# Layer 1 attention: values made in the projection, first maximum packs awaited by row group, key packs issued half a step sooner

## The chip, the cores and the metric

The kernel runs on one core of one Trainium2 chip. The metric is the time on the device in microseconds. An engine of the core is TensorE (PE, its weight loads are PEld), VectorE (DVE), ScalarE (ACT), GpSimd (POOL) or SyncE (SP); SP issues all DMAs of this kernel.

## The reference, cut to what matters

Two transformer layers run one after the other on 2 x 1024 tokens of width 128: attention, normalization, a mixture of experts, normalization, twice. The change is in the attention of layer 1, with 16 heads of 8 channels:

```
q = x @ W_q
k = x @ W_k
v = x @ W_v
latent_kv = (k + v) @ W_down_kv
k_rec = (latent_kv @ W_up_k).reshape(b, s, H, HD).transpose(0, 2, 1, 3)
v_rec = (latent_kv @ W_up_v).reshape(b, s, H, HD).transpose(0, 2, 1, 3)
scores = jnp.einsum('bhqd,bhkd->bhqk', qh, k_rec) / math.sqrt(d)
decay = jnp.exp(-LAMBDA_DECAY * jnp.abs(t[:, None] - t[None, :]))
attn = jax.nn.softmax(scores * decay[None, None, :, :], axis=-1)
out = jnp.einsum('bhqk,bhkd->bhqd', attn, v_rec)
```

## The kernel before

**Projection** (project_l1, line 868). The tokens are taken in four groups of 512. PE makes queries (line 922), the sum of keys and values (918, 919), its 32 latent rows (931) and the keys (935). ACT copies the sum and the latent out, the latent into a part of PR, the tile that later holds the exponentials. DVE multiplies queries and keys by the two decay factors (983; four planes w for each group), and every plane is cut into three bf16 parts: ACT rounds the first (949), DVE subtracts it (988), ACT rounds the second (953), POOL makes the third (998). For groups 0 and 1, which are batch 0, this ends here and SP writes the parts to DRAM (q_parts, k_parts; 895). For groups 2 and 3 only the first part is made, and the rests stay in PR (`rest`); second and third parts follow in the attention (1424 and 1281, tile `late`).

After the first and second parts have landed, SP's program for the projection issues the key and query packs of the first maximum step (`mp.load_k`, 12 DMAs, lines 1065 and 1068, tile KM; `mp.load_q`, 8 DMAs, line 1055, tile QM) and then eight stores of third parts (895). The projection is a block of its own: no engine begins the next block before all engines have ended theirs.

**Attention** (attention_l1, line 1072). An *iteration* `it` (0 to 7) is four heads of one batch; a *half step* `h` (0 to 15) is one half of its queries, and `h = 2 it` is the even one. In each half step there are NT = 9 groups `g` of four heads, so g runs from 0 to 143. PE makes the scores of a group (1347) from the packs QP and KP, ACT takes the exponential (1434) into PR, POOL masks the diagonal (1290), and two groups later PE multiplies by the values V (1366) into OUT. The row maximum that goes into the exponent is made ahead: for each half step 16 *maximum tiles* of 128 x 1024 products on PE (1316) that DVE reduces at once (1446); DVE negates and splits the 16 columns (1455, 1458), PE turns them (1325), DVE copies them out (1467, tile MT), and SP writes them as two rows into QP (1190, `max_rows(h)`). The first scores of half step h wait for these rows, and those of an even one also for the packs. PE runs 22 maximum tiles (LEAD) before the first scores, then two in most groups.

**In these 22 tiles** PE also makes the values: 16 blocks of 128 tokens by 144 columns, three in one PSUM bank, so six fills (`values`, 1375), which ACT copies into V (1420). After them it runs 56 products of the identity by itself that nothing reads (`keep_busy`, 1381).

**SP's queue in the attention** has one order: wait for the stored third parts, rows of ones for KP (1231), the packs KP (5 DMAs, 1178) and QP (6 DMAs, 1166) of iteration 0, QM of iteration 1, `max_rows(0)`, KM of iteration 1, `max_rows(1)`. Then for each half step h: the stored sums of h-1 (1195), fetches of earlier results (1205, 1207) and inverses (1214, 1220), in an even half step QP of the next iteration (6 DMAs), in an odd one its KP (5 DMAs; for iteration 1 both in half step 0), then `max_rows(h + 1)`, late parts, and in an even half step QM and KM of the iteration after the next (20 DMAs).

Of the kernel before, what the change touches and what calls it, by code (L numbers as in the profile page):

```python
# [22 lines left out]
ALU = mybir.AluOpType  # L23
# [844 lines left out]
def project_l1(nc, X, t, mp, late, PR, QS, KS):  # L868

    NV = 4  # L870
    with ExitStack() as ctx:
        sb, pb, sem = sbuf(nc, ctx), psum(nc, ctx), Sems(nc, ctx)
        W, DEC = t["W"], t["DEC"]
        lat, rest = PR[0:DL + 1, 2].rearrange("p j c -> p (j c)"), PR[:, 0:2].rearrange("p s w c -> p w s c")
        loaded, dec_loaded, first_stored, stored = (t[n] for n in ("loaded", "dec_loaded", "first_stored", "stored"))
        kv = sb("p1_kv", [P, TOK], F32)
        val = sb("p1_val", [P, NV, 2, GW], F32)
        early = sb("p1_early", [P, NV, NPART, S], BF16)
        psQ, psKV, psK = ([pb(f"p1_{n}{s}") for s in range(2)] for n in ("psQ", "psKV", "psK"))
        psL = pb("p1_psL")  # L880
        q_ready, kv_ready, kv_read, lat_ready, lat_read, k_ready, val_done, rest_done, part1, part2, part3, ones_set = (
            sem(f"p1_{n}") for n in ("q_ready", "kv_ready", "kv_read", "lat_ready", "lat_read", "k_ready",
                                     "val_done", "rest_done", "part1", "part2", "part3", "ones_set"))
# [4 lines left out]
        def part(g, w, i):  # L888
            return (early, late)[g // 2][:, w, i, g % 2 * GW:(g % 2 + 1) * GW]

        with nc.Block() as block:  # L891
            @block.sync
            def _(sp):
                def store(g, w, i, done):
                    sp.dma_start((QS if w < 2 else KS)[:, w % 2, i, :, grp(g)], part(g, w, i)).then_inc(done, 16)

                for g in range(2):
                    for w in range(NV):
                        for i, written in enumerate((part1, part2)):
                            sp.wait_ge(written, g * NV + w + 1)  # L900
                            store(g, w, i, first_stored)
                sp.wait_ge(first_stored, 2 * NV * 2 * 16)
                mp.load_k(sp, 0)
                mp.load_q(sp, 0)
                for g in range(2):
                    for w in range(NV):
                        sp.wait_ge(part3, g * NV + w + 1)
                        store(g, w, 2, stored[0])

            @block.tensor  # L910
            def _(pe):
# [11 lines left out]

                first(0)
                for g in range(NG):
                    if g + 1 < NG:
                        first(g + 1)
                    pe.wait_ge(kv_read, g + 1)
# [6 lines left out]
                    nc.tensor.matmul(psK[g % 2][:], W["upk"][:], lat[0:DL, grp(g)], start=True, stop=True).then_inc(k_ready, 1)  # L935

            @block.scalar
            def _(act):
# [15 lines left out]

                copy_kv(0)
                for g in range(NG):
# [3 lines left out]
                    else:  # L960
                        first_part(g, 0)
                    if g + 1 < NG:
                        copy_kv(g + 1)
# [6 lines left out]
                    if g < 2:  # L970
                        second_part(g, NV - 1)

            @block.vector
            def _(dve):
                dve.wait_ge(dec_loaded, 16)
                for g in range(NG):
                    pos = slice((g % 2) * GW, (g % 2 + 1) * GW)
                    for w in range(NV + 1):
# [5 lines left out]
                        if w:  # L984
# [7 lines left out]
            def _(pool):  # L992
                nc.gpsimd.memset(lat[DL:DL + 1, :], 1.0).then_inc(ones_set, 1)
                pool.wait_ge(ones_set, 1)
                for g in range(2):
                    for w in range(NV):
                        pool.wait_ge(part2, g * NV + w + 1)
                        nc.gpsimd.tensor_tensor(part(g, w, 2), rest[:, w, g % 2], part(g, w, 1), ALU.subtract).then_inc(part3, 1)

# [35 lines left out]
class MaxPacks:  # L1035


    Q_LOADS, K_LOADS = 8 * 16, 12 * 16

    def __init__(self, nc, ctx, QS, KS):  # L1040
# [5 lines left out]
        self.k_loaded = [sem(f"km_loaded{s}") for s in range(2)]  # L1046

    def load_q(self, eng, it):

        b, q, s = it // NQUAD, it % NQUAD, it % 2  # L1050
        for g in GROUPS:
            heads = slice(q * HQ + g // 2 * 2, q * HQ + g // 2 * 2 + 2)
            for r in range(2):
                rows = slice(g * MROWS + r, (g + 1) * MROWS, 2)
                eng.dma_start(self.Q[s][rows].rearrange("r h a t -> r (h a) t"), self.QS[heads, :, 0:2, :, b * S:(b + 1) * S].rearrange("h a i d t -> (i d) (h a) t"))\
                    .then_inc(self.q_loaded[s], 16)

    def load_k(self, eng, it):

        b, q, s = it // NQUAD, it % NQUAD, it % 2  # L1060
        for g in GROUPS:
            heads = slice(q * HQ + g // 2 * 2, q * HQ + g // 2 * 2 + 2)
            tok = slice(b * S + g % 2 * GW, b * S + (g % 2 + 1) * GW)
            r0 = g * MROWS
            eng.dma_start(self.K[s][r0:r0 + MROWS:2].rearrange("r h a t -> r (h a) t"), self.KS[heads, :, 0:2, :, tok].rearrange("h a i d t -> (i d) (h a) t"))\
                .then_inc(self.k_loaded[s], 16)
            for i in range(2):
                eng.dma_start(self.K[s][r0 + 1 + i * 2 * HD:r0 + (i + 1) * 2 * HD:2].rearrange("r h a t -> r (h a) t"), self.KS[heads, :, 1 - i, :, tok].rearrange("h a d t -> d (h a) t"))\
                    .then_inc(self.k_loaded[s], 16)


def attention_l1(nc, t, mp, late, PR, ones16, QS, KS, OD, RD, OC):
# [15 lines left out]
    FILL = GW // VW  # L1088
    NFILL = -(-B * KB // FILL)
# [9 lines left out]
    def tiles_until_turn(h):  # L1099

        return issued(turn_group(h) - 1) if h else NTILE + 2
# [3 lines left out]
    def tile_slot(m):  # L1105

        return m + sum(tiles_until_turn(h) <= m for h in range(NHALF))

# [25 lines left out]
    with ExitStack() as ctx:  # L1134
# [3 lines left out]
        COR, ID, WV, stored = (t[n] for n in ("COR", "ID", "WV", "stored"))  # L1138
        V = sb("a1_V", [P, B * KB, VW], F32)
        lat, rest = PR[0:DL + 1, 2].rearrange("p j c -> p (j c)"), PR[:, 0:2].rearrange("p s w c -> p w s c")  # L1140
        junk = sb("a1_junk", [P, 2, S], BF16)
        OST = [sb(f"a1_OST{s}", [P, GW], F32) for s in range(2)]
        SPREAD = sb("a1_SPREAD", [P, 2, GW], F32)
# [11 lines left out]
        ones_loaded, out_clear, s_filled, s_read, m_filled, m_read, masked, pv_done, out_read, neg_done, m_rows, inverse_done, scaled, mid_done, low_done, v_ready, v_kept = (  # L1155
            sem(n) for n in ("ones_loaded", "out_clear", "s_filled", "s_read", "m_filled", "m_read", "masked", "pv_done", "out_read",
                             "neg_done", "m_rows", "inverse_done", "scaled", "mid_done", "low_done", "v_ready", "v_kept"))
# [24 lines left out]
        with nc.Block() as block:  # L1182
            @block.sync
            def _(sp):
# [7 lines left out]
                def store(h):  # L1192

                    sp.wait_ge(out_read, h + 1)
                    sp.dma_start(OD[h], OST[h % 2][:]).then_inc(out_stored[h % 2], 16)
# [32 lines left out]

                sp.wait_ge(stored[0], 2 * 4 * 16)
# [3 lines left out]
                load_pack_q(sp, 0)  # L1233
                mp.load_q(sp, 1)
                max_rows(0)
                mp.load_k(sp, 1)
                max_rows(1)
                for h in range(NHALF):
# [11 lines left out]
                    if it + 1 < NIT:  # L1250
# [4 lines left out]
                        if h % 2 == (it >= 1):  # L1255
# [40 lines left out]
            def _(pe):  # L1296
# [5 lines left out]
                def max_tile(m):  # L1302
                    h, i, k = m // NTILE, m % NTILE, tile_slot(m)
                    it, s = h // 2, h // 2 % 2
                    row, j = h % 2 * 4 + i // HQ, MAX_ORDER[i % HQ]
                    if h % 2 == 0 and i == 0:
                        pe.wait_ge(mp.q_loaded[s], (it // 2 + 1) * mp.Q_LOADS)
                        pe.wait_ge(mp.k_loaded[s], (it // 2 + 1) * mp.K_LOADS)
# [61 lines left out]
                def values(f):  # L1370

                    if f >= NRING:
                        pe.wait_ge(v_kept, f - NRING + 1)
                    for n in range(f * FILL, min(f * FILL + FILL, B * KB)):
                        last = nc.tensor.matmul(ring[f % NRING][:, n % FILL * VW:(n % FILL + 1) * VW], lat[:, n * P:(n + 1) * P], WV[:],
                                                start=True, stop=True)
                    last.then_inc(v_ready, 1)

                def keep_busy(n):

# [548 lines left out]
```

## Time and profile before

| | |
|---|---|
| median of 3 runs | 1486.66 us (1485.92 to 1486.88) |
| the profiled execution | 1490.03 us, its span 1488.3 us |
| PE busy | 1293.4 us (87% of the span) |
| DVE busy | 1131.8 us (76%) |
| ACT busy | 907.9 us (61%) |
| POOL busy | 476.7 us (32%) |
| mean granted TensorE clock | 0.932 |
| layer 1 projection | 749 to 794 us of the span |
| layer 1 attention | 794 to 1227 us |

Times of the trace count from the span's start. An engine's idle time is put before the instruction that ended it, with the releaser. PEclk is 1.00 at 2.4 GHz and 0.50 at 1.2 GHz. A row of SPq is the issue of a DMA and not its transfer; "landing" is the time from a DMA's issue to its completion. A wait for several semaphores is put down to one of them.

### The profile page before, as it was taken

How to read it: one execution, taken by the hardware profiler on the slowest of the kernel's cores; microseconds unless marked ns; L12 is line 12 of the kernel's file. 1: busy time of each engine (PE TensorE's matmuls, PEld its weight loads, DVE VectorE, ACT ScalarE, POOL GpSimd, SP SyncE). 2: the span in 40 equal slices, each digit the busy share in tenths (PEclk: the TensorE clock that was granted, in tenths of full speed). 3: DMA queues.
4: the chain of work that ended last, by engine and by line, in shares of the span. 5: the costliest groups of instructions: out<-in, count | busy, mean ns of one | idle time of the engine just before them, and what ended most of it. 6: DMA issues, size and time to landing. Idle time of an engine off the chain costs nothing. (4 is left out here: it accounts for less than half of the span.)

```text
span 1488.3 us, 23429 instructions
## 1 busy us (share of the span) xinstructions
PE 1293.4 (87%) x7928; PEld 736.6 (49%) x7928; DVE 1131.8 (76%) x1741; ACT 907.9 (61%) x1502; POOL 476.7 (32%) x988
## 2 busy tenths in 40 slices
PE   4299889608999999999876999899999968999998
PEld 1133333406778778787623222232222316877776
DVE  4266766287999999999665788788898736688885
ACT  3188887104555555555442487788888854767774
POOL 4254545003333343433132242244223422121210
PEclk9599999758999999999985899999999998999999
DMA  4423230005666666666227075443442201022200
GB/s 136 123 54 103 56 102 8 7 14 132 152 147 154 141 156 145 155 148 146 97 78 153 19 160 133 117 102 93 112 113 62 59 26 59 6 99 82 85 29 29
DMA packets 72157, 141.09 MB, mean 95 GB/s; under 512 B 13132, under 2 KB 45197, under 8 KB 65133
## 3 DMA queue, kind: packets, MB, share of 16 engines
q1 hardware_dynamic: 72048, 139.72, 37.5%
q8 instruction: 59, 0.97, 0.3%
q14 instruction: 50, 0.40, 0.1%
HBM read 121.55 MB, written 16.82 MB: 93 GB/s over the span
## 5 line engine op out<-in xcount | busy, mean ns | idle before, releaser
L1446 DVE CUSTOM_DVE_ANT_0 a_junk<-a_mring,a_COR 128x1024 bf16<-128x1024 f32 x256 | 303.5, 1218 | 61.3 <-PE a_mring L1316 60.8
L1434 ACT ACTIVATE a_PR<-a_ring 128x512 f32<-128x512 f32 x576 | 299.9, 603 | 70.9 <-PE a_ring L1347 70.7
L1290 POOL TENSOR_SCALAR_AFFINE_SELECT a_PR<-a_PR 128x128 f32<-128x128 f32 x512 | 136.4, 297 | 267.6 <-ACT a_PR L1434 267.1
L811 ACT ACTIVATE e_HH<-e_H 128x512 fp32r<-128x512 f32 x184 | 116.5, 633 | 162.5 <-DVE e_H L859 162.4
L1347 PE MATMUL a_ring<-a_QP,a_KP 74*128 74x512 bf16 (+3 forms) x768 | 177.7, 334 | 11.6 <-DMA a_KP<-k_parts 6.2
L415 DVE TENSOR_SCALAR a_PR<-a_PR,a_lo,a_hi 128x1024 f32<-128x1024 f32 (+1 forms) x160 | 122.0, 774 | 77.1 <-ACT a_PR L389 74.4
L389 ACT ACTIVATE a_PR<-a_ring,a_ng 128x1024 f32<-128x1024 f32 (+1 forms) x160 | 155.0, 1033 | 14.8 <-PE a_ring L318 14.1
L1366 PE MATMUL a_OUT<-a_PR,a_V 128*9 128x512 f32 (+3 forms) x1536 | 153.0, 495 | 0.0
L830 DVE TENSOR_TENSOR e_HL<-e_H,e_HH 128x512 fp32r<-128x512 f32 x138 | 140.8, 1021 | 13.2
L1347 PEld LDWEIGHTS a_ring<-a_QP,a_KP 74*128 74x128 bf16 x768 | 57.0, 98 | 168.1 <-ACT a_PR L1434 123.1
L1716 DVE TENSOR_TENSOR e_HL<-e_GL,e_HH 128x512 fp32r<-128x512 f32 x144 | 108.4, 757 | 38.2 <-ACT e_HH L1684 34.5
L753 POOL TENSOR_TENSOR e_HL<-e_H,e_HH 128x512 fp32r<-128x512 f32 x46 | 78.8, 1712 | 181.6 <-ACT e_HH L811 181.6
L291 POOL TENSOR_SCALAR_AFFINE_SELECT a_PR<-a_PR 128x128 f32<-128x128 f32 x256 | 98.5, 410 | 110.6 <-DVE a_PR L415 110.6
L1677 ACT ACTIVATE e_GL<-e_psF,e_BF 128x512 f32<-128x512 f32 x144 | 99.2, 690 | 54.2 <-PE e_psF L1635 53.9
L859 DVE TENSOR_TENSOR e_H<-e_T,e_ROUTE 128x512 f32<-128x512 f32 x176 | 122.1, 694 | 1.5
L853 DVE TENSOR_TENSOR e_T<-e_SG,e_psU 128x512 f32<-128x512 f32 x176 | 119.4, 678 | 1.2 <-PE e_psU L769 1.1
L804 ACT ACTIVATE e_SG<-e_psG 128x512 f32<-128x512 f32 x184 | 108.6, 590 | 16.5 <-PE e_psG L769 16.4
L1316 PE MATMUL a_mring<-a_KM,a_QM 32*128 32x512 bf16 (+3 forms) x704 | 80.9, 336 | 20.9 <-PEq L891 15.7
L338 PE MATMUL a_OUT<-a_PR,a_V 128*32 128x256 f32 (+1 forms) x1280 | 88.6, 371 | 10.3 <-DVE a_OALL L420 10.3
L318 PE MATMUL a_ring<-a_QP,a_KP 128*128 128x512 bf16 (+3 forms) x384 | 87.9, 331 | 9.1 <-ACT a_PR L389 8.8
L767 PE MATMUL e_psG<-e_XH,e_WH 128*128 128x512 f32 x184 | 72.4, 393 | 8.5 <-POOL e_WL L748 8.5
L778 PE MATMUL e_acc<-e_HH,e_WH 128*128 128x512 f32 x184 | 76.5, 416 | 2.7 <-POOL e_HL L753 2.4
(232 smaller groups left out, 2308.9 us busy)
## 6 DMA issues: line engine op xcount, KB each, us to landing
e_ROUTE<-routing SPq DMA_DIRECT2D x24, 704.0 KB
a_QP<-q_parts SPq DMA_DIRECT2D x72, 192.0 KB
e_RAW<-in_w_chunks SPq DMA_DIRECT2D x46, 192.0 KB, 7.5
a_QM<-q_parts SPq DMA_DIRECT2D x64, 128.0 KB, 2.9
e_GATE<-gates SPq DMA_DIRECT2D x8, 1024.0 KB, 4.8
e_ROUTE<-routing SPq DMA_DIRECT2D x8, 640.0 KB
a_KP<-k_parts SPq DMA_DIRECT2D x24, 192.0 KB
e_ROUTE<-routing SPq DMA_DIRECT2D x8, 576.0 KB
```

Source lines behind the costliest of these rows:

```text
L389: nc.scalar.activation(PR[T][:, j, 0:WIDTH0[T]], ring[n % RING][:, 0:WIDTH0[T]], ACT.Exp, scale=ng[:, head]).then_inc(ring_read, 1)
L415: nc.vector.tensor_scalar(p, p, lo[:, head], hi[:, head], ALU.max, ALU.min).then_inc(clamped, 1)
L804: nc.scalar.activation(SG[n % 2][:], psG[n % 2][:], ACT.Silu).then_inc(silu_done, 1)
L811: nc.scalar.activation(HH[n % NH][:], HT[n % NH][:], ACT.Copy).then_inc(high_done, 1)
L830: nc.vector.tensor_tensor(HL[n % NH][:], HT[n % NH][:], HH[n % NH][:].bitcast(F32), ALU.subtract)\
L853: nc.vector.tensor_tensor(T[n % 2][:], SG[n % 2][:], psU[n % 2][:], ALU.mult).then_inc(mul_done, 1)
L859: nc.vector.tensor_tensor(HT[n % NH][:], T[n % 2][:], ROUTE[c % NW][:, grp(g)], ALU.mult).then_inc(h_ready, 1)
L1290: last = nc.gpsimd.affine_select(out=d, in_=d, compare_op=keep, fill=0.0, base=0, pattern=[[step, P]], channel_multiplier=-step)
L1347: last = nc.tensor.matmul(ring[n % NRING][:, a - h % 2 * GW:b - h % 2 * GW], KP[s][:, j, var, kb * P:(kb + 1) * P], QP[s][:, h % 2, j, var ...
L1366: last = nc.tensor.matmul(OUT[j * HP:j * HP + VC, a:b], V[:, b0 + kb, v0:v0 + VC], PR[:, g % NPR, j, a:b], start=(T == 0), stop=(T == NT - ...
L1434: nc.scalar.activation(PR[:, g % NPR, j, :], ring[n % NRING][:], ACT.Exp).then_inc(s_read, 1)
L1446: nc.vector.tensor_tensor_reduce(out=junk[:, i % 2, :], in0=mring[k % 2][:], in1=COR[:, c:c + S], scale=1.0, scalar=-3.0e38, op0=ALU.mult, ...
```

## The change

1. **Values.** PE makes the six fills inside the projection: two before the last latent product, four after the last key product, in PSUM banks of the projection; ACT copies them there. V, `late` and PR belong to both blocks (class SharedL1).
2. **No unread products.** `keep_busy` and its waits are gone from the 22 tiles; the turn of the first maxima comes one tile sooner.
3. **Rests of group 2** are subtracted by POOL at the end of its program instead of by DVE.
4. **First maximum packs.** They are loaded by row group (two heads and half of the keys' tokens), 3 DMAs of KM and 2 of QM each, with a semaphore each. Groups 0 and 1 (10 DMAs) are issued in the projection, groups 2 and 3 (10 DMAs) at the start of the attention, before the eight stores of third parts, which move out of the projection (`store_third`). The 16 tiles of half step 0 are taken head by head (`row_and_head`), so the first eight need only groups 0 and 1.
5. **Other order on SP.** `max_rows(0)` comes before QM of iteration 1. KP of the next iteration follows its QP in the even half step.
6. **A table load sooner.** ACT takes one exponential of a single column (`warm`) before its first group.
7. The third parts share their memory with the tiles OST and SPREAD (`area`).

The core of the diff:

```diff
-                mp.load_k(sp, 0)
-                mp.load_q(sp, 0)
                 for g in range(2):
-                    for w in range(NV):
-                        sp.wait_ge(part3, g * NV + w + 1)
-                        store(g, w, 2, stored[0])
+                    mp.load_first(sp, g)
...
                 for g in range(NG):
                     if g + 1 < NG:
                         first(g + 1)
+                    else:
+                        pe.wait_ge(ones_set, 1)
+                        values(0)
+                        values(1)
...
+                for f in range(2, NFILL):
+                    if f >= 4:
+                        pe.wait_ge(v_kept, f - 3)
+                    values(f)
...
-                        if w:
+                        if w and g != 2:
                             dve.wait_ge(part1, g * NV + w)
...
+                for w in range(NV):
+                    pool.wait_ge(part1, 2 * NV + w + 1)
+                    pool.wait_ge(part3, w + 1)
+                    nc.gpsimd.tensor_tensor(rest[:, w, 0], val[:, w, 0], part(2, w, 0), ALU.subtract).then_inc(rest_pool, 1)
...
+                for g in range(2, 4):
+                    mp.load_first(sp, g)
+                store_third(sp, t, shared, QS, KS)
                 sp.wait_ge(stored[0], 2 * 4 * 16)
...
                 load_pack_k(sp, 0)
                 load_pack_q(sp, 0)
+                max_rows(0)
                 mp.load_q(sp, 1)
-                max_rows(0)
                 mp.load_k(sp, 1)
...
                             load_pack_q(sp, it + 1)
-                        if h % 2 == (it >= 1):
                             load_pack_k(sp, it + 1)
...
+        return h % 2 * 4 + (i // HQ if h else i % 4), (MAX_ORDER[i % HQ] if h else i // 4)
...
+                    if h == 0 and i % 8 == 0:
+                        for half in range(2):
+                            pe.wait_ge(mp.first_loaded[i // 8 * 2 + half], mp.FIRST_LOADS)
...
-                    if m < NFILL:
-                        values(m)
-                    else:
-                        pe.wait_ge(v_kept, NFILL)
-                        for n in range(3):
-                            keep_busy(n)
-                for n in range(8):
-                    keep_busy(n)
...
+                act.wait_ge(cor_loaded, 32)
+                nc.scalar.activation(warm[:], COR[:, 0:1], ACT.Exp)
```

**SP at the seam between projection and attention.** Before, from the end of the early stores to the packs of iteration 0 (the branches end and begin a block):

```order
L895 DMA k_parts<-p_early 16x8x512 x4
L1065 DMA a_KM<-k_parts 16x4x512
L1068 DMA a_KM<-k_parts 8x4x512 x2
...
L1055 DMA a_QM<-q_parts 16x4x1024 x8
L895 DMA q_parts<-p_early 16x8x512 x2
...
L895 DMA k_parts<-p_early 16x8x512 x2
L891 UNCONDITIONAL_BRANCH
...
L1231 DMA a_KP<-in_ones 2x8192 x2
```

The same place in the changed kernel (a_area holds the third parts):

```order
L925 DMA k_parts<-p_early 16x8x512 x4
L1136 DMA a_KM<-k_parts 16x4x512
L1139 DMA a_KM<-k_parts 8x4x512 x2
L1127 DMA a_QM<-q_parts 16x4x1024 x2
...
L1127 DMA a_QM<-q_parts 16x4x1024 x2
L921 UNCONDITIONAL_BRANCH
...
L1136 DMA a_KM<-k_parts 16x4x512
...
L1127 DMA a_QM<-q_parts 16x4x1024 x2
L888 DMA q_parts<-a_area 16x8x512 x2
...
L888 DMA k_parts<-a_area 16x8x512 x2
L1307 DMA a_KP<-in_ones 2x8192 x2
```

Ten loads and eight stores have moved from the left of the block's end to its right, ahead of the packs.

**SP in an even half step, h = 4.** Before (a_MT is the source of `max_rows(5)`):

```order
L1214 DMA o_inverse<-a_INV 32x64
L1220 DMA a_SPREAD<-o_inverse 32x1x512
L1166 DMA a_QP<-q_parts 24x8x512 x6
L1190 DMA a_QP<-a_MT 1x32x128 x2
L1055 DMA a_QM<-q_parts 16x4x1024 x8
```

In the changed kernel:

```order
L1287 DMA o_inverse<-a_INV 32x64
L1293 DMA a_area<-o_inverse 32x1x512
L1239 DMA a_QP<-q_parts 24x8x512 x6
L1251 DMA a_KP<-k_parts 24x8x1024
L1251 DMA a_KP<-k_parts 16x8x1024
L1251 DMA a_KP<-k_parts 8x8x1024 x2
L1251 DMA a_KP<-k_parts 16x8x1024
L1263 DMA a_QP<-a_MT 1x32x128 x2
L1127 DMA a_QM<-q_parts 16x4x1024 x8
```

The five DMAs of KP, which stood in front of `max_rows(h + 1)` in the odd half steps, now stand in front of it in the even ones, behind QP's six.

**PE at the end of the projection**, in the changed kernel with its waits; before, the two products of p_psL and p_psK followed each other and nothing came after them:

```order
L972 MATMUL p_psK<-a_PR,p_upk 128x512 [waits p1_val_done,p1_lat_read]
L953 MATMUL p_psV<-p_WV,a_PR 128x144 [waits p1_ones_set]
L953 MATMUL p_psV<-p_WV,a_PR 128x144 x2
L953 MATMUL p_psKV<-p_WV,a_PR 128x144 x3
L968 MATMUL p_psL<-p_kv,p_down 32x512 [waits p1_lat_read,p1_kv_read]
L972 MATMUL p_psK<-a_PR,p_upk 128x512 [waits p1_val_done,p1_lat_read]
L953 MATMUL p_psKV<-p_WV,a_PR 128x144 x3
L953 MATMUL p_psL<-p_WV,a_PR 128x144 x3
L953 MATMUL p_psV<-p_WV,a_PR 128x144 [waits p1_v_kept]
```

Six small products now stand before the last latent product and ten after the last key product.

## Rows read from the trace of the kernel before

**Rows 1.** Timeline, 770 to 795 us: start, length, engine, line, tiles, count [idle, releaser].

```profile
775.30 0.62 SPq L1065 DMA_DIRECT2D a_KM<-k_parts  x1
...
783.57 5.05 SPq L1055 DMA_DIRECT2D a_QM<-q_parts  x8
...
792.53 1.24 SPq L895 DMA_DIRECT2D k_parts<-p_early  x2
...
794.61 0.61 PE L1316 MATMUL a_mring<-a_KM,a_QM 32*128 32x128 bf16 x3 [15.73 <-PEq L891]
```

**Rows 2.** Timeline, 793 to 850 us, the first maxima until the first exponential.

```profile
795.15 1.80 PE L1375 MATMUL a_ring<-p_WV,a_PR 33*128 33x144 f32 x6
...
795.54 0.58 SPq L1231 DMA_DIRECT2D a_KP<-in_ones  x2
796.17 3.55 SPq L1178 DMA_DIRECT2D a_KP<-k_parts  x5
...
799.76 4.79 SPq L1166 DMA_DIRECT2D a_QP<-q_parts  x6
...
804.60 6.23 SPq L1055 DMA_DIRECT2D a_QM<-q_parts  x8
...
814.12 1.22 DVE L1446 CUSTOM_DVE_ANT_0 a_junk<-a_mring,a_COR 128x1024 bf16<-128x1024 f32 x1
...
815.27 1.22 DVE L1446 CUSTOM_DVE_ANT_0 a_junk<-a_mring,a_COR 128x1024 bf16<-128x1024 f32 x1
...
831.38 0.81 PE L1347 MATMUL a_ring<-a_QP,a_KP 74*128 74x512 bf16 x3
...
831.85 1.28 ACT L1434 ACT_TABLE_LOAD   x1 [23.11 <-PE a_ring L1347]
```

**Rows 3.** Line 1055 from 783 to 789 us, its landing line.

```profile
DMA to landing us min/median/max: 2.7/2.9/3.0
```

**Rows 4.** Line 1055 from 809.6 to 811 us, the same line.

```profile
DMA to landing us min/median/max: 9.9/10.4/11.0
```

**Rows 5.** Window, length, busy PE, PEld, DVE, ACT, POOL, PEclk, DMA share, GB/s.

```profile
838.00:842.00 4.00, 3.90 (x20) 0.73 (x20) 3.00 (x6) 1.44 (x3) 1.99 (x8) 0.50 0.01 4
```

**Rows 6.** Timeline of PE, the transposes that turn the maxima (line 1325).

```profile
851.87 0.29 PE L1325 MATMUL a_mring<-a_ID,a_neg_part 128*32 128x128 bf16 x2
...
921.78 0.28 PE L1325 MATMUL a_mring<-a_ID,a_neg_part 128*32 128x128 bf16 x2
951.74 0.29 PE L1325 MATMUL a_mring<-a_ID,a_neg_part 128*32 128x128 bf16 x2
975.09 0.28 PE L1325 MATMUL a_mring<-a_ID,a_neg_part 128*32 128x128 bf16 x2
```

**Rows 7.** Timeline of PE, first score products of four half steps.

```profile
933.85 1.44 PE L1347 MATMUL a_ring<-a_QP,a_KP 74*128 74x512 bf16 x3 [5.18 <-DMA a_KP<-k_parts]
...
958.60 0.82 PE L1347 MATMUL a_ring<-a_QP,a_KP 74*128 74x512 bf16 x3
...
982.46 0.81 PE L1347 MATMUL a_ring<-a_QP,a_KP 74*128 74x512 bf16 x3 [0.45 <-DMA a_KP<-k_parts]
...
1029.77 0.81 PE L1347 MATMUL a_ring<-a_QP,a_KP 74*128 74x512 bf16 x3 [0.56 <-DMA a_KP<-k_parts]
```

**Rows 8.** Timeline of SP's queue, 944 to 977 us.

```profile
944.22 4.83 SPq L1166 DMA_DIRECT2D a_QP<-q_parts  x6
952.43 1.22 SPq L1190 DMA_DIRECT2D a_QP<-a_MT  x2
...
970.61 3.48 SPq L1178 DMA_DIRECT2D a_KP<-k_parts  x5
975.78 1.21 SPq L1190 DMA_DIRECT2D a_QP<-a_MT  x2
```

**Rows 9.** Line 1190 from 952 to 954 us, its landing line.

```profile
DMA to landing us min/median/max: 1.8/1.8/1.9
```

**Rows 10.** Line 1190 from 975 to 978 us, its landing line.

```profile
DMA to landing us min/median/max: 4.8/5.4/6.0
```

More of the change, by code:

```diff
@@ L870, in project_l1, with store_third @@
+def store_third(sp, t, shared, QS, KS):
+    for g in range(2):
+        for w in range(4):
+            at = slice(g * GW, (g + 1) * GW)
+            sp.dma_start((QS if w < 2 else KS)[:, w % 2, 2, :, at], shared.third[:, w, at]).then_inc(t["stored"][0], 16)
+def project_l1(nc, X, t, mp, shared, QS, KS):
     NV = 4
+    FILL = GW // VW
+    NFILL = -(-B * KB // FILL)
     with ExitStack() as ctx:
         sb, pb, sem = sbuf(nc, ctx), psum(nc, ctx), Sems(nc, ctx)
-        W, DEC = t["W"], t["DEC"]
@@ L879, in project_l1 @@
         psQ, psKV, psK = ([pb(f"p1_{n}{s}") for s in range(2)] for n in ("psQ", "psKV", "psK"))
[L880 to L883, printed above, removed]
+        psL, psV = pb("p1_psL"), pb("p1_psV")
@@ L888, in part @@
         def part(g, w, i):
-            return (early, late)[g // 2][:, w, i, g % 2 * GW:(g % 2 + 1) * GW]
+            at = slice(g % 2 * GW, (g % 2 + 1) * GW)
+            if g >= 2:
+                return late[:, w, i, at]
+            return early[:, w, i, at] if i < 2 else shared.third[:, w, at]
         with nc.Block() as block:
@@ L922, in first, with values @@
                     nc.tensor.matmul(psQ[g % 2][:], W["wq"][:], xg, start=True, stop=True).then_inc(q_ready, 1)
+                def values(f):
+                    for n in range(f * FILL, min(f * FILL + FILL, B * KB)):
+                        last = nc.tensor.matmul(fills[f][:, n % FILL * VW:(n % FILL + 1) * VW], lat[:, n * P:(n + 1) * P], WV[:],
+                                                start=True, stop=True)
+                    last.then_inc(v_ready, 1)
                 first(0)
@@ L971, in _ @@
                         second_part(g, NV - 1)
+                for f in range(2, NFILL):
+                    keep_values(f)
             @block.vector
@@ L1046, in __init__ @@
         self.k_loaded = [sem(f"km_loaded{s}") for s in range(2)]
+        self.first_loaded = [sem(f"m_first_loaded{g}") for g in range(4)]
     def load_q(self, eng, it):
-        b, q, s = it // NQUAD, it % NQUAD, it % 2
[L1051 to L1056, printed above, removed]
@@ L1072, in attention_l1, with load_k, load_first, load_q_group @@
-def attention_l1(nc, t, mp, late, PR, ones16, QS, KS, OD, RD, OC):
+        for g in GROUPS:
+            self.load_q_group(eng, it, g, self.q_loaded[it % 2])
+    def load_k(self, eng, it):
+        for g in GROUPS:
+            self.load_k_group(eng, it, g, self.k_loaded[it % 2])
+    def load_first(self, eng, g):
+        self.load_k_group(eng, 0, g, self.first_loaded[g])
+        self.load_q_group(eng, 0, g, self.first_loaded[g])
+    def load_q_group(self, eng, it, g, arrived):
+        b, q, s = it // NQUAD, it % NQUAD, it % 2
+        heads = slice(q * HQ + g // 2 * 2, q * HQ + g // 2 * 2 + 2)
+        for r in range(2):
+            rows = slice(g * MROWS + r, (g + 1) * MROWS, 2)
+            eng.dma_start(self.Q[s][rows].rearrange("r h a t -> r (h a) t"), self.QS[heads, :, 0:2, :, b * S:(b + 1) * S].rearrange("h a i d t -> (i d) (h a) t"))\
+                .then_inc(arrived, 16)
@@ L1099, in tiles_until_turn @@
     def tiles_until_turn(h):
-        return issued(turn_group(h) - 1) if h else NTILE + 2
+        return issued(turn_group(h) - 1) if h else NTILE + 1
     turn_slots = [tiles_until_turn(h) + h for h in range(NHALF)]
@@ L1368, in weigh @@
                     last.then_inc(pv_done, 1)
[L1370 to L1379, printed above, removed]
-                    nc.tensor.matmul(ring[n % NRING][:], ID[:], ID[:].unsqueeze(1).to_broadcast([P, GW // P, P]), start=True, stop=True)
                 pe.wait_ge(cor_loaded, 32)
@@ L1848, in build @@
                 packs = MaxPacks(nc, part, q1, k1)
[L1849 to L1851 removed]
+                shared = SharedL1(nc, part)
+                project_l1(nc, X, consts1, packs, shared, q1, k1)
+                attention_l1(nc, consts1, packs, shared, a["ones16"], q1, k1, o1, r1, OC1)
             early = ahead_l1(nc, moe)
```

94 lines of the change are left out of this document (54 added, 40 removed).

## Prediction

> **What bounds the kernel now.** I read the page first (PE is busy 87% of the span, so the question is where it is not), then the waits of the stretch around the start of layer 1's attention, then the timeline of PE and of SP's queue there, and last PE's timeline at the half steps. Three things are to be seen.
>
> First, at the seam nobody computes: PE stood idle for 15.73 us until 794.61, so its last product of the projection ended at 778.9 [rows 1]. What ended last there is SP: it issued the first loads of KM at 775.30, QM from 783.57, eight stores until 792.53 + 1.24 = 793.8, and the block ended 0.8 us later [rows 1]. The loads' data weren't waited for: QM landed 2.7 to 3.0 us after issue [rows 3].
>
> Second, the lead of 22 maximum tiles runs from 794.6 to the first scores at 831.38, 36.8 us [rows 2]. Each fill of the values keeps PE for 1.80 us between two tiles [rows 2]. Later two reductions of DVE begin 1.15 us apart [rows 2], which is DVE's own pace, and at that pace 22 tiles need 25 us. The packs went out early: KP from 796.17, QP from 799.76 [rows 2].
>
> Third, in the steady part the turns of the maxima are 23.35 us apart (951.74 to 975.09), but 29.96 us from 921.78 to 951.74 [rows 6]. In that interval PE waited 5.18 us at 933.85, and at two later even half steps 0.45 and 0.56 us [rows 7]. The profile puts all three to KP. But the two rows of `max_rows`, issued behind KP at 975.78 to 977.0, took up to 6.0 us, so they landed at 982.4, just where PE went on [rows 7, 8, 10]; with only QP ahead of them, at 952.43, they took 1.8 to 1.9 us [rows 8, 9]. So these rows queue behind KP.
>
> **The seam.** SP keeps 10 of its 20 loads. The 20 took from 775.30 to 788.62, 0.67 us each [rows 1], so SP ends at 782.0, and with the 0.8 us of the seam the first tile could come at 782.8. PE gets ten blocks of values behind its last key product: at 1.80 us for three, at the half clock [rows 2], 6 us, so 784.9, with ACT's copy and the seam 786.2. At the full clock it is half, and SP is last. The six blocks ahead of the last latent product take up to 3.6 us; I set them against the wait that PE has there now for ACT's copies, and if that cover fails the seam moves by at most 2 us. POOL's four subtractions end before SP does and free DVE. I take the first tile at 783.5: 11.1 us sooner (8.4 to 11.8).
>
> **The lead.** Values and unread products go, so DVE sets the pace: 22 tiles at 1.15 us, the negation and the turn (about 1 us) end the lead at 783.5 + 26.5 = 810 or a little later. The second eight tiles need row groups 2 and 3: ten issues of 0.67 us from 783.5 and 3 us of landing give 793.2; tile 8 is due at 783.5 + 0.8 + 8 x 1.15 = 793.5. Nothing is lost there, a microsecond at most.
>
> What is late next is the packs. Ahead of them SP now has ten loads (6.7 us) and eight stores (793.8 - 788.6 = 5.1 us), then the 1.8 us between the last store and the ones (793.8 to 795.54) [rows 1, 2]. So the ones go out at 783.5 + 13.6 = 797.1, which is 1.6 us **later** than before, though the block starts 11 us sooner. When the packs landed no row says, for nobody waited. The last QM of iteration 1, issued at 810.2 behind them, landed 11.0 us later, at 821.2 [rows 2, 4]. Packs (2304 KB) and this QM (1024 KB) thus took from about 797.5 to 821.2; by bytes the packs had landed at 813.9. After: 815.5, less a little since QM no longer follows at once; I take 814.5. Both ends: 810.5 (the packs never wait) and 821. The first scores come at 814.5 instead of 831.38, **16.9 us** sooner (10 to 21).
>
> From the first score to the turn of half step 1 it was 851.87 - 831.38 = 20.5 us [rows 2, 6]. In it lie the table load of 1.28 us [rows 2], which goes (ACT takes it while it waits), and a stretch at the half clock: PEclk is 0.50 in 838 to 842 us, after the gap of the table load, with PE busy for 3.90 of 4.00 us [rows 5]. After the change PE reaches the first scores out of a thinner lead and a wait of some 4 us, so this stretch should come at once. A pause of 5.18 us cost 29.96 - 23.35 = 6.6 us [rows 6, 7], so 1.4 us beside itself. I set the table load against the colder start: 0, from +2 to -4.
>
> **Key packs in the even half step.** Gain: the 6.6 us of the long interval, 0.45 and 0.56 us: **7.6 us**. Price: `max_rows(h + 1)` in the even half steps now stands behind KP. At 944.22 QP's six go out until 949.05; KP's five follow until 952.5, and the rows at once, hardly later than now. In the odd half step KP went out from 970.61 and the rows were there at 982.4, 11.8 us later [rows 8, 10]. From 949.05 that is 960.9. PE wants them at 958.60 [rows 7]: a stall of 2.3 us. If QP's data, still moving, hold KP up, it is more (4 us); if the rows slip through at their unloaded 1.8 us, it is none. I take 2 us in the five half steps 5 to 13 and 1 us in half step 3, where QP goes out a little earlier relative to the turn: **11 us** (0 to 24). PE is busy nearly throughout here, so a stall is not made up. The balance is -3.4 us, from +7.6 to -16.
>
> By the Trainium skill, "DMA: Bandwidth & Descriptors", section "Queues, rings and completion order", each engine consumes its ring in order and a completion is written only after that engine's earlier writes; the rows' 6.0 us behind KP against 1.9 us without agree [rows 9, 10]. Its table "Specifications" gives about 27 GiB/s per DMA engine; with 96 KB on the busiest engine, by its section "Why a DMA increments its semaphore by 16 and not by 1", KP would take some 3.5 us, an estimate by which the rows would be in time. The measured 11.8 us speak against it, and I go by them.
>
> **Sum.** 16.9 - 3.4 = 13.5 us. The profiled execution took 1490.03 us, its span 1488.3 us; it becomes 1476.5 us. It lies 3.4 us above the median of 1486.66 us, which is a matter of the execution and not of the change, so the median becomes 1473.2 us.
>
> **Rivals.** *No new stall behind KP.* For it: the rows go out 6 us before PE wants them (952.6 against 958.60) and need 1.9 us unloaded [rows 7, 9]; against it, the 6.0 us behind KP [rows 10]. Then 16.9 + 7.6 = 24.5 us: 1462 us.
>
> *The lead waits longer for the packs.* For it: the ones go out 1.6 us later although all else is sooner, and the by-bytes share may be too kind since KP moves slower than QM. First scores at 820 and 2 us more of half clock: gain 9.4, balance -3.4: 1481 us.
>
> *Slower.* The rows behind QP and KP: every one of the six even half steps ends in a stall long enough to bring the half clock as well. It decides from (16.9 + 7.6) / 6 = 4.1 us for each; at 5.18 us and 1.4 us of clock as at 933.85 [rows 6, 7] it is 39 us against 24.5: 1501 us. Against it: rows 8 give 2.3 us where KP alone is ahead.
>
> *It doesn't do what it says.* If PE's ten blocks of values and the copies pushed the seam back to where it was and the packs were equally late, only KP's balance would be left: 1487 to 1490 us. Nothing in rows 1 holds the seam but SP.
>
> **How the numbers follow.** My forecast has 0.55; no new stall 0.2; longer wait for packs 0.17; slower 0.05; no effect 0.03. The likeliest gives 1473.2 us, and its own range, with 10 to 21 us for the lead and a balance between 0 and -7, is 1466 to 1481. A measurement of this kernel can tell 0.2%, 3 us, from no change. Toward 1462 the first rival reaches, so the range is 1461 to 1481. Faster by over 3 us: the forecast and the first two rivals nearly whole, 0.92; within 3 us 0.03; slower 0.05.
>
> **What would show it.** In the changed profile: PE's idle time at the seam 4 to 5 us instead of 15.73, with SP or the values as the last; no line 1381; DVE's tiles 1.15 us apart from the first; the first exponential at about 815, PE waiting before it for the packs by some 4 us; the idle time of 5.18 us at the even half step 4 gone; instead idle times of 1 to 3 us before the first scores of half steps 3, 5, 7, 9, 11 and 13, and the rows' landing there 7 to 9 us instead of 1.9. I am wrong if those stalls are missing (faster than 1466), or if they exceed 4 us each.

## The result, and the profile after

| | before | changed |
|---|---|---|
| median | 1486.77 us (1485.92 to 1490.6, 4 runs) | 1519.28 us (1506.58 to 1520.03, 4 runs) |
| ratio | | 1.0176, 95% interval 1.0138 to 1.0214 |
| profiled execution, its span | 1490.03 us, 1488.3 us | 1518.71 us, 1517.0 us |

The change made the kernel slower; forecast were 1473.2 us, and a range of 1461 to 1481. In the runs below, one execution of k_back (1861.74 us) and one of the kernel before (1985.01 us) ran at a mean granted clock of about 0.6 and are left out of medians and ratios. The page names the place in two rows, its first and the group of the score products. The last columns of such a group are PE's idle time just before it and what ended most of it:

```profile
span 1517.0 us, 23320 instructions
...
L1426 PE MATMUL a_ring<-a_QP,a_KP 74*128 74x512 bf16 (+3 forms) x768 | 183.5, 343 | 47.5 <-DMA a_QP<-a_MT 43.8
```

The 47.5 us were 11.6 us before. The DMA named is a_QP<-a_MT, the two rows of the maxima, not a pack.

**The seam** did what was forecast. The timeline of the changed kernel there:

```profile
780.34 0.62 SPq L1136 DMA_DIRECT2D a_KM<-k_parts  x1
...
785.83 1.23 SPq L1127 DMA_DIRECT2D a_QM<-q_parts  x2
...
788.17 0.68 PE L953 MATMUL p_psKV<-p_WV,a_PR 33*128 33x144 f32 x2
788.42 0.53 ACT L1000 ACTIVATE a_V<-p_psV 128x432 f32<-128x432 f32 x1 [0.91 <-PE p_psV L953]
788.90 0.29 ACT L1000 ACTIVATE a_V<-p_psKV 128x144 f32<-128x144 f32 x1
789.44 0.56 SPq L1136 DMA_DIRECT2D a_KM<-k_parts  x1
...
789.64 1.04 PE L1395 MATMUL a_mring<-a_KM,a_QM 32*128 32x128 bf16 x6 [0.78 <-PEq L921]
```

All times here lie some 5 us later than before, because this execution lost 4.9 us ahead of layer 1 (its first key product of the projection began at 754.38 instead of 749.47; in the runs below that have the same code up to there it is 747.2 to 751.3, so this is a matter of the execution); so I count from the first load of KM. From there to the first maximum tile it is 9.3 us; it was 19.3 [rows 1]. SP was through at 787.1; the last were the values' products, at the half clock (PEclk 0.50 in 786 to 789.5 us), and ACT's copies, which ended at 789.2.

**The start of the attention.** SP's queue and PE:

```profile
802.93 0.57 SPq L1307 DMA_DIRECT2D a_KP<-in_ones  x2
803.54 3.55 SPq L1251 DMA_DIRECT2D a_KP<-k_parts  x5
807.14 4.79 SPq L1239 DMA_DIRECT2D a_QP<-q_parts  x6
811.97 1.25 SPq L1263 DMA_DIRECT2D a_QP<-a_MT  x2
813.26 5.67 SPq L1127 DMA_DIRECT2D a_QM<-q_parts  x8
```

```profile
814.76 0.61 PE L1395 MATMUL a_mring<-a_KM,a_QM 32*128 32x512 bf16 x3 [0.54 <-DVE a_top L1499]
827.00 1.44 PE L1426 MATMUL a_ring<-a_QP,a_KP 74*128 74x512 bf16 x3 [11.63 <-DMA a_QP<-a_MT]
```

The landing line of the two rows issued at 811.97:

```profile
DMA to landing us min/median/max: 10.5/12.4/14.2
```

The last tile of the lead began at 814.76, and PE then waited 11.63 us, until the second row, issued at 812.6, had landed 14.2 us later. Before, these rows took 1.9 us. The first scores come 46.7 us after the first KM load instead of 56.1: 9.4 us sooner, where 16.9 were forecast.

**The half steps.** PE's first score products of half steps 3, 5, 7, 9, 11 and 13 of the changed kernel:

```profile
900.97 0.82 PE L1426 MATMUL a_ring<-a_QP,a_KP 74*128 74x512 bf16 x3 [2.01 <-DMA a_QP<-a_MT]
...
955.69 1.46 PE L1426 MATMUL a_ring<-a_QP,a_KP 74*128 74x512 bf16 x3 [6.85 <-DMA a_QP<-a_MT]
...
1011.31 1.46 PE L1426 MATMUL a_ring<-a_QP,a_KP 74*128 74x512 bf16 x3 [7.28 <-DMA a_QP<-a_MT]
...
1068.87 1.46 PE L1426 MATMUL a_ring<-a_QP,a_KP 74*128 74x512 bf16 x3 [6.58 <-DMA a_QP<-a_MT]
...
1123.16 1.46 PE L1426 MATMUL a_ring<-a_QP,a_KP 74*128 74x512 bf16 x3 [6.13 <-DMA a_QP<-a_MT]
...
1174.80 1.06 PE L1426 MATMUL a_ring<-a_QP,a_KP 74*128 74x512 bf16 x3 [3.33 <-DMA a_QP<-a_MT]
```

The pause before half step 4 [rows 7] is gone, and six new ones are there, 32.2 us in all. How long the rows travelled is seen at half step 7. SP's queue in half step 6, and the rows' landing line:

```profile
989.59 4.83 SPq L1239 DMA_DIRECT2D a_QP<-q_parts  x6
994.79 3.52 SPq L1251 DMA_DIRECT2D a_KP<-k_parts  x5
998.35 1.22 SPq L1263 DMA_DIRECT2D a_QP<-a_MT  x2
```

```profile
DMA to landing us min/median/max: 8.8/10.6/12.3
```

Issued at 998.35 and 999.0, the second was there at 1011.3, when PE went on. The turns of the maxima show what a pause costs with what follows it (line 1404 of the changed kernel):

```profile
973.72 0.29 PE L1404 MATMUL a_mring<-a_ID,a_neg_part 128*32 128x128 bf16 x2
997.16 0.28 PE L1404 MATMUL a_mring<-a_ID,a_neg_part 128*32 128x128 bf16 x2
...
1031.96 0.29 PE L1404 MATMUL a_mring<-a_ID,a_neg_part 128*32 128x128 bf16 x2
```

From 997.16 to 1031.96 it is 34.8 us instead of 23.35 [rows 6], 11.4 us for a pause of 7.28. The rest goes with the clock: in the windows behind the pause (columns as in [rows 5]) PE is busy without a gap, but at the half clock until about 1020, and at the full one again from 1024:

```profile
1011.30:1016.00 4.70, 4.69 (x19) 0.78 (x20) 2.38 (x4) 2.17 (x4) 0.00 (x0) 0.50 0.49 143
1016.00:1020.00 4.00, 4.00 (x19) 0.59 (x18) 2.34 (x4) 2.17 (x4) 0.00 (x0) 0.50 0.00 0
1020.00:1024.00 4.00, 4.00 (x24) 0.87 (x23) 2.14 (x5) 3.16 (x6) 0.00 (x0) 0.79 0.25 86
1024.00:1028.00 4.00, 3.90 (x29) 0.83 (x27) 3.52 (x7) 3.30 (x8) 0.58 (x2) 1.00 0.08 20
```

**Where the time went**, profiled execution against profiled execution: 5.0 us lost up to the first KM load, 4.9 of them ahead of layer 1, where the change is not; 11.5 us won from the first KM load to the turn of half step 1 (65.1 instead of 76.6 us); 35.7 us lost from that turn (845.41) to the last (1215.49), 370.1 instead of 334.4 us. Together 29.2 us at the last turn; the spans differ by 28.7 us.

### The profile page after: what moved, and what is told of

It is laid out like the page before. It is cut to its first block and busy times, and to the rows that moved or that the text cites. A ratio compares the mean times of both kernels' runs of the same rounds, so it can differ in the third digit from the quotient of the medians.

```text
span 1517.0 us, 23320 instructions
## 1 busy us (share of the span) xinstructions
PE 1292.3 (85%) x7872; PEld 734.1 (48%) x7872; DVE 1128.0 (74%) x1737; ACT 908.3 (60%) x1503; POOL 482.1 (32%) x992
## 5 line engine op out<-in xcount | busy, mean ns | idle before, releaser
L1426 PE MATMUL a_ring<-a_QP,a_KP 74*128 74x512 bf16 (+3 forms) x768 | 183.5, 343 | 47.5 <-DMA a_QP<-a_MT 43.8
L1445 PE MATMUL a_OUT<-a_PR,a_V 128*9 128x512 f32 (+3 forms) x1536 | 157.2, 506 | 0.0
L804 ACT ACTIVATE e_SG<-e_psG 128x512 f32<-128x512 f32 x184 | 108.6, 590 | 16.2 <-PE e_psG L769 16.1
```

The costliest lines, as they stand in the source:

```text
L804: nc.scalar.activation(SG[n % 2][:], psG[n % 2][:], ACT.Silu).then_inc(silu_done, 1)
L1426: last = nc.tensor.matmul(ring[n % NRING][:, a - h % 2 * GW:b - h % 2 * GW], KP[s][:, j, var, kb * P:(kb + 1) * P], QP[s][:, h % 2, j, var ...
L1445: last = nc.tensor.matmul(OUT[j * HP:j * HP + VC, a:b], V[:, b0 + kb, v0:v0 + VC], PR[:, g % NPR, j, a:b], start=(T == 0), stop=(T == NT - ...
```

## The experiments

All are measured beside the kernel before on the same chip (its median is 1491.0 us beside old_start, head_held, lead_busy and third_back, and 1488.4 us beside the others). Two stretches of each profile are put beside each other: from the first load of KM to the first score, and from the turn of half step 1 to the last turn. Each stretch is of one execution. The start before was read three times (56.1, 56.1 and 54.4 us), the changed one four times (45.5 to 46.9 us), so a difference of one or two microseconds there tells nothing; in kernels whose scores never wait for a DMA behind the start, the turns agree within 0.1 us.

| run | median us | ratio to before, 95% | KM to first score | turns |
|---|---|---|---|---|
| before | | | 56.1 | 334.4 |
| changed | 1519.28 | 1.0138 to 1.0214 | 46.7 | 370.1 |
| k_back | 1478.04 | 0.9886 to 0.9947 | 45.5 | 331.5 |
| k_only | 1532.48 | 1.0272 to 1.0326 | 56.1 | 368.3 |
| rows_between | 1471.47 | 0.9870 to 0.9912 | 46.9 | 326.7 |
| qm_held | 1496.24, one run | | 46.0 | 356.0 |
| old_start | 1481.74 | 0.9919 to 0.9969 | 54.4 | 326.7 |
| head_held | 1466.08 | 0.9795 to 0.9866 | 42.7 | 326.7 |
| lead_busy | 1468.92 | 0.9798 to 0.9886 | 46.8 | 326.8 |
| third_back | 1466.49 | 0.9773 to 0.9864 | 41.3 | 326.7 |
| third_again | 1464.55 | 0.9812 to 0.9866 | 41.0 | 326.7 |
| both | 1461.05 | 0.9800 to 0.9848 | 39.7 | 326.7 |

**k_back** undoes one line of the changed kernel.

```diff
                             load_pack_q(sp, it + 1)
+                        if h % 2 == (it >= 1):
                             load_pack_k(sp, it + 1)
```

> The changed kernel with KP of the next iteration back in the odd half steps; all else as changed. Theory A (the rows of the maxima queue behind the packs of the even half step, and this alone costs the 35.6 us that the turns of the changed kernel lose against those of before): the idle times before half steps 5, 7, 9, 11 and 13 are gone, the one of some 5 us before half step 4 is back, and the time is 6 to 12 us under the kernel before, 1475 to 1481 us. Rival B (the new start of the attention, its other order of loads and its shared memory slow the steady part too): the stalls stay, and the time stays over 1500 us.

1478.0 us. The turns take 331.5 us; the pauses of the odd half steps are gone and the old one before half step 4 is back, shorter:

```profile
921.21 0.81 PE L1427 MATMUL a_ring<-a_QP,a_KP 74*128 74x512 bf16 x3 [3.49 <-DMA a_KP<-k_parts]
```

Theory A holds, rival B falls: the new start costs the steady part nothing. The profile names KP here, but the second row of the maxima, issued behind it, landed at 921.2, which is when PE went on.

**k_only** is the kernel before with the other half:

```diff
                             load_pack_q(sp, it + 1)
-                        if h % 2 == (it >= 1):
                             load_pack_k(sp, it + 1)
```

> The kernel before with one edit alone: KP of the next iteration follows QP in the even half step. Theory A: stalls of 6 to 8 us before half steps 5, 7, 9 and 11 as in the changed kernel, 3 us or less before 3 and 13, the 5.18 us before half step 4 gone; the time is 1515 to 1525 us, slower than the changed kernel by what its start gains. Rival B: within 5 us of the kernel before, since the start is the old one.

1532.5 us, 7.5 us above what theory A allowed (its profiled execution took 1522.55 us); why is open. The pauses before half steps 5, 7, 9 and 11 are 5.1 to 7.0 us, where 6 to 8 were expected, and the one before 13 is 3.8 us. The turns take 368.3 us, 33.9 more than before, with the old start. All the same, rival B, which had it within 5 us of the kernel before, is out. The pause before half step 5:

```profile
959.88 1.46 PE L1346 MATMUL a_ring<-a_QP,a_KP 74*128 74x512 bf16 x3 [7.04 <-DMA a_QP<-a_MT]
```

So the loss belongs to this one line of the change.

**rows_between** keeps KP in the even half step but issues it after the rows:

```diff
                             load_pack_q(sp, it + 1)
-                            load_pack_k(sp, it + 1)
+                            if h == 0:
+                                load_pack_k(sp, it + 1)
                     if 0 < h < NHALF - 1:
                         max_rows(h + 1)
+                    if h % 2 == 0 and h and it + 1 < NIT:
+                        load_pack_k(sp, it + 1)
```

> The changed kernel with the two rows of the maxima issued between QP and KP in the even half steps (KP behind them, still half a step sooner than in the kernel before). Theory A: the rows land 1.9 us after issue in every even half step from 4 on, no stall before any half step but the first; the time is the kernel before less 11 us of the start and less 7.6 us of KP: 1466 to 1472 us. Rival C (it is the transfer of KP in the even half step that collides with QM and KM, wherever the rows stand): PE then waits for KM or QM in its maximum tiles or DVE starves, and the time stays above 1485 us.

1471.5 us. SP's queue in an even half step, and the landing line of its two rows:

```profile
972.69 4.83 SPq L1239 DMA_DIRECT2D a_QP<-q_parts  x6
980.96 1.20 SPq L1263 DMA_DIRECT2D a_QP<-a_MT  x2
982.21 3.57 SPq L1251 DMA_DIRECT2D a_KP<-k_parts  x5
```

```profile
DMA to landing us min/median/max: 1.8/1.8/1.8
```

The turns take 326.7 us, 7.6 us less than before and 43.3 less than in the changed kernel, and no score product behind the first waits for a DMA any more. Rival C falls: the same transfers in the same half step cost nothing when the rows go first. The five loads of KP, 1152 KB, go out right behind the rows here and do not slow them. Issuing KP sooner was worth the 7.6 us that the forecast gave it; the place in the queue was wrong.

**old_start** is that order in the kernel before, with its own start.

```diff
-                        if h % 2 == (it >= 1):
+                        if h == 0:
                             load_pack_k(sp, it + 1)
                     if 0 < h < NHALF - 1:
                         max_rows(h + 1)
+                    if h % 2 == 0 and h and it + 1 < NIT:
+                        load_pack_k(sp, it + 1)
```

> The kernel before with its own start, and KP issued in the even half step behind the rows of the maxima. If the gain of KP is what the long turns of the kernel before lost (6.6 us, 0.5 and 0.6 us), the time is 7 to 8 us under the kernel before: 1479 us. If the gain needs the new start, it is nothing.

1481.7 us beside 1491.0 us, and again 326.7 us for the turns: the gain of KP does not need the new start.

**qm_held** asks what the rows share the engines with: in the changed kernel, SP waits for their landing before it issues QM and KM.

```diff
                         sp.wait_ge(m_read, tile_slot((h + 2) * NTILE - 1) + 1)
+                        if h:
+                            sp.wait_ge(m_rows, (h + 2) * 32)
```

> The changed kernel, but in the even half steps SP issues QM and KM only after the rows of the maxima have landed. Theory A (the rows wait for what was issued ahead of them): their landing stays at 9 to 12 us after issue and the time at about 1519 us. Rival D (they share the engines with the 20 loads issued behind them, which run beside them): the landing falls to 4 to 7 us and the time by 15 us or more.

1496.2 us in its one execution, so both theories hold in part. Of the 22.6 us between the two profiled spans, 14.0 lie in the turns; 8.8 lie ahead of the first KM load, where no edit is. Half step 7 again, SP, its rows' landing line and PE:

```profile
981.66 3.48 SPq L1251 DMA_DIRECT2D a_KP<-k_parts  x5
985.18 1.22 SPq L1263 DMA_DIRECT2D a_QP<-a_MT  x2
994.13 5.08 SPq L1127 DMA_DIRECT2D a_QM<-q_parts  x8
```

```profile
DMA to landing us min/median/max: 6.9/7.6/8.2
```

```profile
994.11 0.82 PE L1428 MATMUL a_ring<-a_QP,a_KP 74*128 74x512 bf16 x3 [3.24 <-DMA a_QP<-a_MT]
```

With nothing issued behind them the rows still take up to 8.2 us, 4.1 us less than in the changed kernel; for the rows of half steps 5, 9 and 11 it is 2.5 to 3.4 us less. Of the delay over the 1.9 us of [rows 9], some 6 us are thus the packs ahead and 2.5 to 4.1 us the loads behind.

The changed kernel has the same control in itself: in half step 12 no QM and KM follow.

```profile
1157.30 4.84 SPq L1239 DMA_DIRECT2D a_QP<-q_parts  x6
1162.19 3.48 SPq L1251 DMA_DIRECT2D a_KP<-k_parts  x5
1165.71 1.38 SPq L1263 DMA_DIRECT2D a_QP<-a_MT  x2
...
1181.85 0.33 SPq L1268 DMA_DIRECT2D o_sums<-a_area  x1
```

```profile
DMA to landing us min/median/max: 7.3/7.8/8.2
```

What the packs ahead do is seen when one counts from KP's first issue to the moment at which PE goes on, in the half steps where PE waited for these rows:

| kernel, and PE before half step | ahead of KP | behind the rows | us |
|---|---|---|---|
| before, 4, 6 and 8 | KM, until 3 us before | nothing or eight stores | 11.2, 11.9, 12.5 |
| qm_held, 5, 7, 9 and 11 | QP | nothing | 13.0, 12.5, 13.7, 12.4 |
| changed, 3 and 13 | QP | eight stores; nothing | 12.7, 12.6 |
| changed, 5, 7, 9 and 11 | QP | the 20 loads | 16.4, 16.5, 16.2, 15.7 |

QP, issued 4.8 us ahead of KP, adds about 1 us at most; the 20 loads behind add 3.3 us on the mean.

**head_held** tests the same at the start, on rows_between.

```diff
                 max_rows(0)
+                sp.wait_ge(m_rows, 32)
                 mp.load_q(sp, 1)
```

> The kernel of the run with the rows between QP and KP, and SP issues QM of iteration 1 only after the rows of half step 0 have landed. Theory A2 (packs and rows of the start share the engines with the eight loads of QM issued behind them, as the even half steps did: landing 8.3 instead of 10.4 us when these were held): the rows of half step 0 land 3 to 6 us sooner than 821, the first scores come at 816 to 819 us, the time is 3 to 5 us under 1471.5 us. Rival (they wait only for the packs ahead): no difference, 1471 us. KM of iteration 1 then goes out some 12 us after the first scores and must land before tile 32; if it doesn't, what was won is lost there.

The queue of SP and the first scores:

```profile
803.24 1.25 SPq L1263 DMA_DIRECT2D a_QP<-a_MT  x2
814.14 5.08 SPq L1127 DMA_DIRECT2D a_QM<-q_parts  x8
```

```profile
814.26 1.44 PE L1430 MATMUL a_ring<-a_QP,a_KP 74*128 74x512 bf16 x3 [7.61 <-DMA a_QP<-a_MT]
```

From the ones to the first score it is 20.1 us instead of 24.2 (794.21 and 797.71 are the ones' times), and from the first KM load 42.7 instead of 46.9: 4 us, as theory A2 had it. The three other executions with this start have 22.9 to 24.1 us from the ones to the first score, so 3 to 4 us is what can be told. The turns, 326.7 us, lost nothing by it.

**third_back** issues the stores of the third parts in the projection again, and so moves the seam.

```diff
                 for g in range(2):
                     mp.load_first(sp, g)
+                sp.wait_ge(part3, 2 * NV)
+                store_third(sp, t, shared, QS, KS)
...
-                store_third(sp, t, shared, QS, KS)
```

> The kernel of the run with the rows between QP and KP, with the eight stores of third parts issued in the projection again, so that the seam comes some 5 us later. If the start is bound by SP's queue and the packs, the first scores come as before this edit (821.9 us of the span, give or take 1.5) and the time stays at 1470 to 1474 us, though every maximum tile is 5 us later. If it is bound by the seam, the time is 5 us longer.

This expectation failed: I had looked for no change or a loss. The first maximum tile came 3.4 us later (12.7 us after the first KM load), and the first score 5.6 us **sooner** (41.3 us). SP, which stands still at the seam until the values are copied and later waits 1.7 to 1.8 us for the stores, did the stores in that time, and the ones went out 19.2 us after the first KM load instead of 22.6. That is 3.4 of the 5.6 us. The other 2.2 us lie between the ones and the first score; here QM goes out 6.7 us after QP's last issue instead of 1.3, which fits head_held but is not tested by itself.

**third_again** repeats it, **both** adds head_held's wait.

> The kernel with the rows between QP and KP and the third parts stored in the projection, once more beside the run with both on one chip: 1464 to 1469 us, the first score 65 us after the first key product of the projection. If the earlier 65.1 us was chance, it is 72 us again.

> The kernel with the rows between QP and KP, the third parts stored in the projection again, and QM of iteration 1 issued after the rows of half step 0 have landed. From the first key product of the projection to the first score it was 72.8 us with the rows between alone, 66.5 us with QM held, 65.1 us with the stores back. If both act on one thing, the packs' landing, the second of them can win only what the first left: PE waited 2.9 us for the rows with the stores back, so 62.5 to 65 us, and 0 to 3 us off the time. Rival: QM and KM of iteration 1, now issued later, come too late for the maximum tiles of the next iteration, and the time rises.

The first score came 41.0 and 39.7 us after the first KM load. Counted as in the expectations, from the first key product of the projection, it is 67.3 us (65 expected) and 65.7 us (62.5 to 65 expected). `both` has the shortest start of all; its time of 1461.05 us and that of third_again, 1464.55 us, have intervals that overlap. Against the kernel before it is 1.5% to 2.0% faster.

**lead_busy** puts unread products back, two after each tile from the eighth and 24 after the last.

> The kernel of the run with the rows between QP and KP, with unread products in the lead again: two after each tile from the eighth, 24 after the last. It asks what the half clock at the first scores costs. If PE comes warm to them, the stretch from the first score to the turn of half step 1, 18.3 us now, shortens by 3 to 5 us and the time is 1467 to 1469 us; if the 24 products end too early or the clock is taken back anyway, it is 1471 us; if they hold the lead up, it is longer than 1471 us.

From the first score to the turn of half step 1 it took 17.5 us instead of 18.3. PE came at the full clock (1.00 in the first row), and lost it again soon after; in the run without these products it is 0.50 in the six microseconds from the first score:

```profile
824.00:830.00 6.00, 4.99 (x36) 1.76 (x35) 4.83 (x9) 5.18 (x11) 3.68 (x14) 1.00 0.25 79
830.00:836.00 6.00, 6.00 (x44) 1.65 (x42) 3.89 (x7) 3.30 (x7) 3.65 (x15) 0.72 0.01 4
```

The expectation for a warm PE had 3 to 5 us. The 0.8 us are no more than the same kernel varies by (third_back and third_again have 20.7 and 22.1 us for this stretch), and the ratios of lead_busy and rows_between overlap. Whether taking the unread products away gained or lost is not shown.

## Why the prediction was wrong, point by point

- **The seam: nearly right.** Forecast 8.2 us from the first KM load to the first tile, measured 9.3. The prediction named the values as the later end of its bounds, and at the half clock they were last.
- **The lead's pace: right.** The last of 22 tiles began at 814.76, 25.1 us after the first.
- **The packs' landing: the place right, the size off.** The step was "I take 814.5", 17.4 us from the ones to the first score; it was 24.1 us. I had shared out 23.7 us by bytes between the packs and a QM behind them, as if the one moved after the other, and so gave the packs 16.4 us. head_held shows that QM slows them: 3 to 4 us of the difference is QM. With nothing behind, the last row still landed 19.2 us after the first pack's issue, and in qm_held's half steps 17.3 to 18.5 us after it. So the share by bytes was too kind to the packs besides, as the rival of the longer wait had it. That rival's first score at 820 was near: 46.7 us after the first KM load is 822.0 in the times of the kernel before.
- **From first score to the turn: nearly right.** Forecast no change; 18.4 instead of 20.5 us. That this is the table load is not shown: third_back and third_again also take it early and have 20.7 and 22.1 us.
- **KP's gain: right.** 7.6 us forecast, 7.6 us shown by rows_between and 7.7 by old_start.
- **KP's price: this step failed and turned the sign.** The forecast charged 11 us (0 to 24) against the gain; it was 43.3 us, the turns of the changed kernel against those of rows_between. "I take 2 us in the five half steps" stood on 11.8 us from KP's first issue to the rows' landing, read in an odd half step, where nothing is issued behind the rows. At half step 7 KP's first issue at 994.79 to PE's going on at 1011.31 is 16.5 us. The prediction named one way to more ("if QP's data, still moving, hold KP up"), but that is the smaller part: QP adds about 1 us at most. What it did not see is that 20 loads, issued right behind the rows in the even half step, slow them: 3.3 us on the mean, by qm_held and by the changed kernel's own half steps 3 and 13. For half step 7 it adds up: 2.3 us as the prediction reckoned, 0.4 since KP went out 5.2 instead of 4.8 us after QP, 0.6 by QP and 4.1 by the loads behind give 7.4; the pause is 7.28 us. The six pauses sum to 32.2 us instead of 11, and to 19.0 us in qm_held.
- **The clock after a pause: left out.** The six intervals between turns with a pause are 43.1 us longer than 23.35, 10.9 more than the pauses. This makes up the rest of the 43.3 us. The row for it was in hand (1.4 us at 933.85) and was used for the start and for the rival, not for the price.
- **The rival on the slower side was the right one**, with chance 0.05. It decided from 4.1 us for each half step; measured were 7.2 us on the mean, and its own figure was 6.6. It was judged by the mildest of its terms. So was the range: by its own terms, 10 us for the lead and -7 for KP, it reaches 1484 us and not 1481, and the -16 that KP's price allowed was left out of it.
- The prediction drew on the Trainium skill, "DMA: Bandwidth & Descriptors", section "Queues, rings and completion order", for the rule that a completion is written after the earlier writes of its engine; the runs agree, for with only the packs ahead the rows needed 8.2 us and in front of KP 1.8. The estimate of 3.5 us for KP from the bandwidth per engine in its section "Specifications", by which the rows would have been in time, did not hold here: from KP's first issue to the rows' landing it is 10.9 us at the least.

Open is by what the loads behind slow the rows, and why KP takes so long. The changed kernel's executions spread from 1506.58 to 1520.03 us, but those of the kernel before spread as far beside old_start, from 1483.47 to 1498.5 us, so this spread asks for no cause of its own.

## What to carry to other kernels

A small DMA that an engine waits for must be priced by all that is in the queue when it is issued, ahead and behind, and not only by the transfer that was moved; put it in front of bulk loads that have time. When a wait is replaced by one at several places, multiply the worst case of one place, with the clock it costs, before calling it unlikely. And where the end of a stage is set by the queue of one engine, ask what leaves that queue's critical stretch before asking when the barrier comes.

## What the runs showed of the hardware

- A pair of DMAs of 8 KB each landed up to 1.9 us after issue when the last 1152 KB in the queue, QP, had gone out from 8.2 us before it [rows 8, 9], up to 6.0 us when it was KP from 5.2 us before it [rows 8, 10], up to 8.2 us when it was QP and KP from 8.8 and 3.5 us before it, and up to 12.3 us when 20 loads were issued behind it as well. Loads issued later on the same queue delayed it by 2.5 to 4.1 us; that I had not expected. They did so only where packs were still moving ahead: in rows_between five loads right behind the pair left it at 1.8 us.
- A pause of PE of 7.28 us in a busy stretch cost 11.4 us, for PE then ran at the half clock until about 1020, 9 us after it; one of 2.01 us before half step 3 cost 3.1 us (turns 26.49 us apart).
- In this kernel a barrier that came 3.4 us later went with a first score 5.6 us sooner, since the queue that bounds the next stage was busy during it.
